# Gate values and three sums ahead of the last relu, the check behind the third group, and five discarded matmuls in each image

## What is computed

```
v = group_norm(x)                                # 32 groups of 16 channels
r = relu(v)
r = where(max_hw(r) - mean_hw(r) < 0.5, 0, r)    # per channel; hardly ever happens
bb = 1 - exp(-|max_c(r) - mean_c(r)|)            # per pixel
y = bb * r
control = sigmoid(pooled @ W1.T) * c3            # pooled = mean_hw(y)
c3 = relu(pooled @ W3.T), 1.2 where that is < 1
out = x + where(y < control * max_hw(y), 0, y)
```

## Time and profile before

| | |
|---|---|
| median of three runs | 1694.12 us (1691.63 to 1694.9) |
| the profiled execution's own time | 1694.59 us |
| its span, first to last instruction | 1692.8 us |
| busy: PE, DVE, ACT, POOL | 75%, 86%, 80%, 36% |
| mean granted TensorE clock | 0.868 of full speed |
| HBM traffic | 310.38 MB read, 205.52 MB written |

### The profile page before, as it was taken

One profiled execution on the slowest core, in us unless ns is written; L12 is line 12 of the kernel. 1 busy time (PEld: TensorE's weight loads), 2 busy tenths in 40 slices (PEclk: granted clock), 3 DMA queues, 4 the chain that ended last, 5 costly groups with the idle time before them and its releaser, 6 DMA issues.

```text
span 1692.8 us, 26138 instructions
## 1 busy us (share of the span) xinstructions
PE 1266.6 (75%) x9888; PEld 883.0 (52%) x9888; DVE 1459.9 (86%) x2192; ACT 1355.9 (80%) x2177; POOL 610.5 (36%) x446
## 2 busy tenths in 40 slices
PE   3788777887777888777788877778877778877761
PEld 1555455555555555455555555555545555555550
DVE  2588889988889898888998888998888989888896
ACT  6788888788888788888878888888888888888821
POOL 0032334442344442244443243443233444224440
PEclk8988888998788998888898888899888899888885
DMA  9259999999999999999999999999999999999973
GB/s 394 112 127 318 340 355 311 291 314 303 338 350 324 287 316 301 339 343 341 299 303 307 316 343 346 299 309 313 311 342 351 318 299 316 292 340 342 302 228 152
DMA packets 93345, 517.64 MB, mean 306 GB/s; under 512 B 10272, under 2 KB 10272, under 8 KB 93216
## 3 DMA queue, kind: packets, MB, share of 16 engines
q1 hardware_dynamic: 75360, 416.38, 61.1%
q0 software_dynamic: 17856, 99.56, 30.1%
HBM read 310.38 MB, written 205.52 MB: 305 GB/s over the span
## 4 chain that ended last, share of the span: by engine, by line
PE 40%; POOL 28%; ACT 20%; DVE 7%; issue 3%; DMA 1%; DVEq 0%; SPq 0%; ACTq 0%
POOL xs L788 25%; PE ps_gate L331 11%; PE ps_gate L298 10%; PE ps_turn L288 8%; ACT rs L482 6%; ACT rs L457 6%; ACT xs L482 4%; PE ps_gate L318 3%; PE ps_gate L360 2%; PE ps_gate L368 2%; POOL rstd L767 2%; PE ps_gate L306 2%; DVE xs L649 2%; ACT junk L433 1%; DVE max_and_mean L632 1%
## 5 line engine op out<-in xcount | busy, mean ns | idle before, releaser
L632 DVE TENSOR_REDUCE max_and_mean<-ps_turn 128x2 f32<-128x1024 f32 x384 | 463.6, 1218 | 31.8 <-PE ps_turn L288 28.1
L288 PE MATMUL ps_turn<-ident,xs 128*128 128x128 f32 (+1 forms) x1600 | 359.6, 311 | 175.2 <-DVE max_and_mean L632 112.0
L788 POOL TENSOR_TENSOR xs<-xs,rs 128x1568 f32<-128x1568 f32 x124 | 433.3, 3531 | 1.8 <-DVE rs L680 1.8
L779 POOL DMA_DIRECT2D xs<-in_x x124 | 111.5, 968 | 889.4 <-DVE xs L680 796.9
L433 ACT ACTIVATE junk<-xs 128x1568 bf16<-128x1568 f32 x256 | 385.4, 1505 | 9.8 <-ACT junk L433 0.4
L318 PE MATMUL ps_gate<-ident,bb 128*128 128x128 f32 (+1 forms) x1600 | 272.2, 332 | 156.3 <-ACT bb L475 150.8
L288 PE MATMUL ps_turn<-ident,rs 128*128 128x128 f32 (+1 forms) x1600 | 345.7, 302 | 0.0
L318 PEld LDWEIGHTS ps_gate<-ident,bb 128*128 128x128 f32 (+1 forms) x1600 | 248.8, 239 | 175.9 <-DVE ymax_parts L649 163.7
L288 PEld LDWEIGHTS ps_turn<-ident,xs 128*128 128x128 f32 (+1 forms) x1600 | 209.0, 155 | 248.2 <-DVE max_and_mean L632 158.4
L649 DVE CUSTOM_DVE_ANT_0 xs<-xs,ps_gate 128x768 f32<-128x768 f32 (+1 forms) x256 | 243.1, 958 | 48.7 <-PE ps_gate L318 48.5
L457 ACT ACTIVATE xs<-xs,shift,rstd 128x3136 f32<-128x3136 f32 x64 | 192.0, 3001 | 86.0 <-POOL shift L771 80.8
(11 more groups left out here) (80 smaller groups left out, 955.7 us busy)
## 6 DMA issues: line engine op xcount, KB each, us to landing
xs<-in_x SPq DMA_DIRECT2D x260, 784.0 KB, 13.7
out<-xs SPq DMA_DIRECT2D x256, 784.0 KB, 8.2
xs<-in_x POOLq DMA_DIRECT2D x124, 784.0 KB, 10.9
rs<-in_L_conv_W SPq DMA_DIRECT2D x2, 1024.0 KB, 17.5
```

Of the source, the lines that this page charges most:

```text
L288: mm = pe.transpose(ps_turn[0:w, n % 2, b - 2 * i, P * t:P * (t + 1)], r_tile(s, t)[:, P * b:P * b + w], ident[:, :])
L632: ins = dve.tensor_reduce(max_and_mean[:, 2 * i:2 * i + 2, 0], ps_turn[:, n % 2, :, :], AX.X, ALU.max)
L779: pool.dma_start(half(x_tile(s - 1, t), h), dram_half(x_tiles, s - 1, t, h), accum_op=ALU.add).then_inc(x_added[(s - 1) % XR][t][h], 16)
L788: pool.tensor_tensor(o, o, half(r_tile(s - 1, t), h), ALU.add).then_inc(added, 1)
```

## The change

Five edits:

1. The squares of tiles 1 to 3 in load order are one ACT operation each in place of two halves; only the first tile loaded keeps its halves. The values themselves are discarded into `junk`, which becomes fp8 in place of bf16 (only the accumulated sum is used). `copy_mean_rows` and `copy_means` move one tile of squares back.
2. `row_means` is scaled by a negative number, so that POOL's `affine` needs one small operation less (`mrs` goes).
3. On ACT, `pool_sum(s, 0, 0)` to `pool_sum(s, 0, 2)` and `gate_values(s, 3)` go ahead of the last relu of the next image; `pool_sum(s, 0, 3)` follows that relu.
4. On DVE, `peaks` goes behind `gate(s, 2, 3)`, and `settle_channels` right behind `read_count`, so that three gates of group 3 follow the branch instead of two.
5. On TensorE, `keep_clock` makes discarded 512-column matmuls: two behind `spread(s, 2)`, two behind `spread(s, 3)`, one behind `count_fails(s + 1)`.

```diff
+            def keep_clock(s, n):
+                pe.wait_ge(t_read, NT * s + NT - 1)
+                for _ in range(n):
+                    pe.matmul(ps_turn[:, NT * (s + 1) % 2, 0, :], ident[:, :], wt[:, 0, 0, :], start=True,
+                              stop=True, skip_group_check=True)
...
                 spread(s, 2)
+                keep_clock(s, 2)
                 spread(s, 3)
                 if s + 1 < B:
+                    keep_clock(s, 2)
                     count_fails(s + 1)
+                    keep_clock(s, 1)
...
-            def square_half(s, n, h):
+            def square(s, t, cols, part):
+                junk_step.wait()
+                junk_step.step(act.activation(junk[:, cols], x_tile(s, t)[:, cols], ACT.Square,
+                                              scale=float(HW) ** -0.5, accum_out=squares[:, part:part + 1],
+                                              saturate=False))
...
                 if has_next:
                     square_tile(s + 1, 1)
+                    square_tile(s + 1, 2)
                 copy_mean_rows(s)
                 if has_next:
-                    square_tile(s + 1, 2)
+                    square_tile(s + 1, 3)
                 copy_means(s)
                 if has_next:
-                    square_tile(s + 1, 3)
                     row_means(s + 1)
...
                 gate_values(s, 2)
-                pool_sum(s, 0, 0)
+                for t in range(3):
+                    pool_sum(s, 0, t)
+                gate_values(s, 3)
                 if has_next:
                     relu(s + 1, RELU_ORDER[3])
-                gate_values(s, 3)
-                for t in range(1, T):
-                    pool_sum(s, 0, t)
+                pool_sum(s, 0, 3)
...
-                gate(s, 2, 0)
-                gate(s, 2, 1)
-                gate(s, 2, 2)
+                for t in range(T):
+                    gate(s, 2, t)
                 if nxt < B:
                     peaks(nxt)
-                gate(s, 2, 3)
-                if nxt < B:
                     margins(nxt)
                     find_fails(nxt)
                 gate(s, 3, 0)
                 if nxt < B:
                     read_count(nxt)
-                gate(s, 3, 1)
-                if nxt < B:
                     settle_channels(nxt)
-                gate(s, 3, 2)
-                gate(s, 3, 3)
+                for t in range(1, T):
+                    gate(s, 3, t)
                 top(s)
...
-                steps.step(pool.tensor_tensor(mrs[:, :], gst[:, 0, :], rstd[:, :], ALU.mult))
-                steps.wait()
-                pool.tensor_scalar(shift[:, :], mrs[:, :], -1.0, 1.0, ALU.mult, ALU.mult).then_inc(affine_ready, 1)
+                pool.tensor_tensor(shift[:, :], gst[:, 0, :], rstd[:, :], ALU.mult).then_inc(affine_ready, 1)
```

More of the change, by code:

```diff
@@ L6 @@
 F32 = mybir.dt.float32
-BF16 = mybir.dt.bfloat16
+FP8 = mybir.dt.float8e4
 I32 = mybir.dt.int32
@@ L82, in gated_sparsifier @@
         wt = sb("wt", [P, 2, T, C])
-        junk = sb("junk", [P, HALF], BF16)
+        junk = sb("junk", [P, HW], FP8)
         rows = sb("rows", [P, C])
@@ L98, in gated_sparsifier @@
         half_neg = sb("half_neg", [P, T])
-        squares = sb("squares", [P, 2, T])
+        squares = sb("squares", [P, T + 1])
         row_sum = sb("row_sum", [P, 1])
@@ L106, in gated_sparsifier @@
         rstd = sb("rstd", [P, T])
-        mrs = sb("mrs", [P, T])
         shift = sb("shift", [P, T])
@@ L342, in group_stats @@
                 pe.matmul(ps_group[:, 0, :], group_pick[:, :], row_mean[:, :], start=True, stop=True)
[L343 to L347, removed]
+                pe.wait_ge(squared, (T + 1) * (s + 1))
+                first = LOAD_ORDER[0]
+                pe.matmul(ps_group[:, 1, :], group_avg[:, :], squares[:, 0:T], start=True, stop=False,
+                          skip_group_check=True)
+                pe.matmul(ps_group[:, 1, first:first + 1], group_avg[:, :], squares[:, T:T + 1],
+                          start=False, stop=True, skip_group_check=True).then_inc(group_sums, 1)
             def count_fails(s):
@@ L427, in _, with square_half, square_tile @@
             junk_step = Steps(act, squared)
-            def square_half(s, n, h):
-                t = LOAD_ORDER[n]
[L431 to L438, removed]
+            def square(s, t, cols, part):
[3 more added lines that the diff above has]
+                                              saturate=False))
+            def square_half(s, h):
+                t = LOAD_ORDER[0]
+                act.wait_ge(x_loaded[s % XR][t][h], 16 * (s // XR + 1))
+                square(s, t, slice(HALF * h, HALF * (h + 1)), t if h == 0 else T)
+            def square_tile(s, n):
+                t = LOAD_ORDER[n]
+                wait_loaded(act, s, t)
+                square(s, t, slice(0, HW), t)
             def row_means(s):
@@ L443, in row_means @@
                 steps.step(act.activation(junk[:, 0:XCHUNK], ps_rowsum, ACT.Identity,
-                                          scale=1.0 / (PER_GROUP * HW), accum_out=row_sum[:, :]))
+                                          scale=-1.0 / (PER_GROUP * HW), accum_out=row_sum[:, :],
+                                          saturate=False))
                 steps.wait()
@@ L492, in _ @@
             act.wait_ge(consts_ready, 1)
-            for n in range(T):
+            for h in range(2):
+                square_half(0, h)
+            for n in range(1, T):
                 square_tile(0, n)
@@ L503, in _ @@
                 if has_next:
-                    square_half(s + 1, 0, 0)
+                    square_half(s + 1, 0)
                 if s > 0:
@@ L507, in _ @@
                 if has_next:
-                    square_half(s + 1, 0, 1)
+                    square_half(s + 1, 1)
                 if s > 0:
```

## The result

The changed kernel takes 1707.64 us (median of four runs, 1706.53 to 1712.35) against 1692.88 for the kernel before in the same rounds (four runs, 1690.36 to 1694.9): ratio 1.0096 [1.0074, 1.0118], about 1% slower. The forecast was 1693, no change that can be told; its range ended at 1707. The profiled execution took 1706.53, its span 1704.7.

What follows compares the result with a forecast made beforehand. DVE's nearly unbroken work, then the chain from first maximum to logits, set the step. 49.2 + 0.75 x 1.6 = 50.4; 30 steps +2.0, last image -3.5, start +0.5: span 1691.8, plus 1.8 is 1693.6, stated as 1693; range 1662 to 1707.

Steps and rivals of the forecast that it cites:

- the step with the clock up: One image, logits copy to logits copy, TensorE keeping its clock: 49.2 us in place of 50.42.
- steps of two kinds: Sign in the profile after: steps near 49.2 us and near 50.8; all of one kind would make the forecast wrong.
- the price of a lost clock: TensorE's turn 2 and products at lowered clock: at least 0.9 us, at most 1.16 plus 2.1; taken as 1.6.
- The start: First image: the last tile's square starts only when both halves are in, 1.3 us later, partly hidden; put at +0.5.
- the last image: Two ACT sums of 1.47 move ahead of gate_values(s, 3), so the last sum ends near 1652: 3.5 us gained, once.
- I take three images in four: TensorE's 2.7 us rest between turn 1 and turn 2: share of images that lose the clock there.
- forecast A: Clock lost between turns 1 and 2 in half to nine of ten images: 1681 to 1701 us; chance 0.56.
- are hidden in the 4.83 us rest: TensorE: two discarded matmuls behind spread 2, ending at 786.2, fit into its idle time before the third spread.
- rival D: Discarded matmuls are in the way: clock down at the third spread, fails counted at 795, over 1730 us; chance 0.08.
- rival C: Clock lost each time, or open branch costs 0.4 more: steps of 50.8 and over, 1705 to 1715 us; chance 0.17.
- Rival B: Clock never or seldom lost between turns 1 and 2: steps of 49.2, 1657 us, up to 1675; chance 0.19.

## Why the prediction was wrong, by its own steps

**What held.** The third spread at 34.2 behind the logits (measured 34.20 to 34.27 in 19 of 30) and 1.8 long (1.94); no DVE wait for it; the gate of group 3 at 38.0 (38.00); 1.1 idle behind the branch (1.10); the first maximum at 43.3 (43.2); 2.7 of rest between turns 1 and 2 (2.41, since the two turns took 1.96 and not 1.7); the step with the clock up 49.2 (49.22); steps of two kinds; one discarded matmul 0.95 (a pair 1.88 to 1.99); the price of a lost clock 1.6 (50.86 - 49.22 = 1.64). On the kernel before, edits 1 and 2 cost and gained nothing. The start came out 0.5 shorter instead of 0.5 longer, and the last image gained 2.6 of the 3.5. The start of the third spread is partly luck: the forecast took it from DVE's gates and gave the whole squares no part in it, but with halved squares, in the same order on ACT, it stands at 34.87. The changed kernel itself was not run with halves.

**The steps that failed** are two. The first is "I take three images in four", the share of images that lose the clock in that rest. It was 26 of 30. That is 26 x 1.64 = 42.6 us in place of 30 x 0.75 x 1.6 = 36: 6.6 more. The bracket was right, a rest of 1.86 on one side and one of 4.83 on the other, but nothing between them had been measured, and three in four was a guess. This share alone does not miss: it gives 1693 + 6.6 = 1699.6, inside the range, and 0.87 of the images is inside forecast A's "half to nine of ten". The other half of the miss is what the sum put at nothing, above all "are hidden in the 4.83 us rest".

**The terms put at nothing.** In 11 of 30 steps the clock was down behind the second spread, and the first discarded pair, taken as hidden in the rest of 4.83, ran at half clock and pushed the third spread by 1.05, the first maximum by 0.37. Edit 3 had shortened the rest that was to hide it, and in these steps the second spread was slow as well: it ended 32.3 behind the copy and not 30.8, and from 32.3 to 34.2 there is room for a pair of 1.9, not for one of 3.1. The prediction's own rows had the clock down just there in 14 of 30 images. That is 10 x 0.37 = 3.7 (the eleventh is the last step). The condition of rival D, a clock that is down at the third spread, did not come; its mechanism did, one spread earlier and at about an eighth of its price. And steps with a late branch (four by some 0.33, the last by 1.6; the kernel before has the like, 0.46 to 0.72 of idle time behind the branch in five steps in place of 0.17) were not in the one step that the forecast was made from: 2.9. Why the branch is late in them is not known. The three make 13.2; the 30 steps (1525.1) passed the forecast (30 x 50.4 = 1512) by 13.1. The misses of the start and the last image cancel.

The result is thus rival C's time, but only half by its reason: the clock was lost nearly each time, and the open branch cost what was forecast (1.10). Rival B fell. The Trainium skill ("TensorE: Matmul & The Clock Gate", "Why this matters for your kernels") warns only of longer pauses between bursts of matmuls; the trace disagrees, with 26 of 30 lost at 2.41. Part 4 of the same page of the Trainium skill says that PE-mode transposes do not count as busy for the clock in the way of other matmuls. Here the trace disagrees too: in the kernel with the gate over the branch and no discarded matmuls, the clock was down when turn 2 began (0.69 for two transposes) and up for the products right behind it (1.90), with only the turn's transposes between.

**Why edits that each did their work made the kernel slower.** Edit 3 brought the third spread to where it should be, and edit 5 kept the third spread at full clock. Edit 4 opened the branch, which costs 0.93 where it stands and leaves TensorE 0.94 more to rest in front of turn 2. Undoing that half of edit 4 takes the changed kernel from 1.0096 to 0.9724 of the kernel before.

**What stays open.** Why the clock, down during the turns in both kernels without discarded matmuls, is back for the products with the gate over the branch and not without it: the rest in front of turn 2 differs (0.43 against 0.70), but so does the place in the step at which the clock first fell (33 to 41 against 28 to 35 behind the copy, once 39), and no run moved one without the other. Nor do the runs show why the same rest of 2.41 costs the clock in one step and not in the next. In the changed kernel the place of the fall drifts: 44.9, 45.3, 45.6 and 45.9 behind the copies of four steps in a row from 508.26 on, and the fifth step keeps its clock. No run moved this place alone, so the counts 26 of 30 and none of 30 hold for these orders, not for the length of a rest by itself. Why loads come late for the whole squares at steps of 49.2 and less (25.0 and 28.6 us of waits with one and three matmuls in the rest, 45.7 with the gate over the branch) was not tried.

## What to carry to other kernels

Look at the last rest of TensorE in front of its longest matmuls on the critical path, and shorten that first: one microsecond of discarded work in it was worth 46 us here, and one gate moved so that it covers the branch and shortens the rest 64. Where an engine waits for a register and a branch, keep an instruction over that wait; its price is not only the engine's own idle time but the rest that it leaves elsewhere. Discarded matmuls with work of the critical path queued behind them must be counted at their price with the clock down, 3.1 for a pair in place of 1.9, since that is when they are there to help. The same five were worth 9 us (1717.04 to 1707.64) and 11 us in two orders and cost 5 in the order of before (ratio 1.003), so they have to be tried in place; and the mean clock of a kernel does not tell whether they helped.

## What the runs showed of the hardware

- In front of turn 2, a rest of 2.41 us cost the clock in 26 of 30 steps, one of 1.55 or 1.47 in none of 30 in three kernels (one matmul in the rest; gate over the branch with whole and with halved squares).
- Discarded fp32 matmuls of 512 columns at 2.4 GHz: one by itself takes 1.02 to 1.13, two take 1.88 to 1.99, three 2.74. Two took 3.12 where the clock was down for most of them.
- From the cast of the flag to the next DVE work behind the branch lie 1.24 us, to the turn that it releases 1.17 (799.48, 800.72, 800.65). One gate of 0.94 over the branch left 0.18 of 1.10 idle.
- ACT's squares with an accumulated sum took 1.51 for 1568 columns and 2.82 for 3136. If the time grows evenly with the columns, 2 x 1.506 - 2.817 = 0.19 of each is fixed (an estimate).
